# Maxima across partitions by turns on TensorE, row sums on ScalarE, keys split ahead, and a projection placed inside the first layer

## The reference

```python
q, k, v = (einsum('blh,dh->bdl', u, W) + b for W, b in ((Wq, bq), (Wk, bk), (Wv, bv)))
k  = causal_conv(k, k_kernel) + k_D[None, :, None] * k       # by FFT of length 1024, first 512 kept
kv = k * v
y  = (causal_conv(kv, ssm_kernel) + kv * D[None, :, None]) * q
x  = layernorm(u + einsum('blh,oh->blo', swapaxes(y, 1, 2), Wo) + bo)
h  = square(relu(einsum('bsd,fd->bsf', x, W_fc)))            # 256 -> 1024
s  = einsum('bsf,df->bsd', h, W_proj)                        # 1024 -> 256
spikes: 5 steps of mem = 0.9 * mem + s - reset; count of mem > 1, divided by 5
out = layernorm(x + spikes / 5)
```

## Time and profile before

| | us |
|---|---|
| median of 3 runs (lowest to highest) | 859.67 (856.86 to 860.92) |
| profiled execution: time, span | 861.3, 859.3 |
| TensorE busy (share of the span) | 743.8 (87%) |
| VectorE busy | 713.3 (83%) |
| ScalarE busy | 529.9 (62%) |
| GpSimd busy | 390.3 (45%) |
| mean granted TensorE clock | 0.962 of full |

### The profile page before, as it was taken

The page is one execution under the profiler, slowest core; times in us unless marked ns, Lnnn a source line. Parts: engine busy times, 40 slices in busy tenths (PEclk is TensorE's granted clock), DMA queues, the critical chain, the costliest instruction groups (busy, mean ns, idle before and its releaser), DMA issues.

```text
span 859.3 us, 26944 instructions
## 1 busy us (share of the span) xinstructions
PE 743.8 (87%) x11392; PEld 545.7 (64%) x11392; DVE 713.3 (83%) x1192; ACT 529.9 (62%) x625; POOL 390.3 (45%) x307
## 2 busy tenths in 40 slices
PE   0067977999999999766699999999999999999993
PEld 0067977999999999765455555555555455555541
DVE  6896755788888888886568999999999999999885
ACT  2382746778878887765255655666555665556661
POOL 0341212223222222322377666876668866677642
PEclk9998988999999999986799999999999999999997
DMA  8994857999999997890100111011110111101001
GB/s 336 342 263 103 189 135 173 210 231 224 222 228 227 226 211 160 187 263 20 49 1 1 50 49 49 5 44 49 49 49 11 37 49 49 49 20 31 25 24 50
DMA packets 55369, 100.71 MB, mean 117 GB/s; under 512 B 5664, under 2 KB 41376, under 8 KB 53280
## 3 DMA queue, kind: packets, MB, share of 16 engines
q1 hardware_dynamic: 53952, 97.94, 44.7%
q10 hardware_dynamic: 1376, 2.23, 0.7%
HBM read 89.92 MB, written 27.01 MB: 136 GB/s over the span
## 4 chain that ended last, share of the span: by engine, by line
PE 44%; DVE 24%; POOL 17%; issue 10%; DMA 2%; ACT 1%; SPq 0%; POOLq 0%; DVEq 0%; ACTq 0%
PE ps L697 16%; PE ps L683 15%; POOL arena L630 14%; DVE arena L1184 7%; PE ps L813 5%; PE ps L820 5%; DVE u_maxima L917 2%; DVE arena L1181 2%; PE ps L794 2%; DVE arena L1141 2%; DVE arena L1166 2%; DVE arena L1160 2%; DVE arena L971 1%; DMA arena<-kpad_dram 1%; PE ps L772 1%
## 5 line engine op out<-in xcount | busy, mean ns | idle before, releaser
L683 PE MATMUL ps<-arena 128*128 128x96 f16 x3072 | 143.2, 211 | 62.2 <-DVE arena L971 50.8
L697 PE MATMUL ps<-arena 128*128 128x64 f16 (+3 forms) x6144 | 172.2, 182 | 23.3 <-issue 8.9
L630 POOL TENSOR_TENSOR arena<-arena 128x512 f16<-128x512 f32 x128 | 178.9, 1429 | 14.9 <-ACT arena L514 14.4
L697 PEld LDWEIGHTS ps<-arena 128*128 128x128 f16 x6144 | 169.7, 97 | 24.5 <-issue 14.7
L683 PEld LDWEIGHTS ps<-arena 128*128 128x128 f16 x3072 | 138.4, 101 | 64.6 <-issue 56.4
L820 PE MATMUL ps<-arena 128*128 128x512 f16 x768 | 173.2, 379 | 2.9 <-POOL arena L630 2.9
L813 PE MATMUL ps<-arena 128*128 128x512 f16 x768 | 170.8, 379 | 3.4 <-DVE arena L1166 2.5
L596 POOL TENSOR_TENSOR arena<-arena 128x512 f16<-128x512 f32 x32 | 38.1, 1190 | 240.4 <-ACT arena L471 240.4
L1173 DVE TENSOR_TENSOR arena<-arena 128x512 f32<-128x512 f32 x128 | 137.7, 1129 | 10.8 <-POOL arena L630 9.0
L510 ACT ACTIVATE arena<-ps,read_factor 128x512 f32<-128x512 f32 x128 | 88.0, 687 | 76.6 <-PE ps L813 59.6
L820 PEld LDWEIGHTS ps<-arena 128*128 128x128 f16 x768 | 74.0, 98 | 90.6 <-POOL arena L630 9.7
(11 more groups left out here) (99 smaller groups left out, 724.9 us busy)
## 6 DMA issues: line engine op xcount, KB each, us to landing
arena<-kpad_dram SPq DMA_DIRECT2D x192, 256.0 KB, 5.8
kpad_dram<-ksplit_dram SPq DMA_DIRECT2D x64, 256.0 KB, 6.2
qy<-in_uT SPq DMA_DIRECT2D x8, 1024.0 KB, 17.2
arena<-in_u SPq DMA_DIRECT2D x16, 512.0 KB, 4.0
out<-arena SPq DMA_DIRECT2D x16, 512.0 KB, 3.0
arena<-in_k SPq DMA_DIRECT2D x2, 512.0 KB, 5.1
ksplit_dram<-arena ACTq DMA_DIRECT2D x2, 512.0 KB, 3.7
arena<-in_wfT SPq DMA_DIRECT2D x1, 1024.0 KB, 8.7
```

Of the source, the lines that this page charges most:

```text
L630: nc.gpsimd.tensor_tensor(h16[:, 1, f], h_square[:, f % 4], h16[:, 0, f], ALU.subtract).then_inc(h_lo, 1)
L683: last = nc.tensor.matmul(o, u16[:, x, t, tok:tok + P], wcur[:, w, t], start=(k == 0), stop=(k == 3 * DT - 1))
L697: last = nc.tensor.matmul(out[:, ch * COL + delta * B:(ch + 1) * COL], taps(c, tp)[:, delta * P:(delta + 1) * P], data[:, xp, ch * COL:ch ...
```

## The change

1. The three `partition_all_reduce` go. In their place TensorE turns the columns of maxima (n columns become n rows), VectorE takes the maximum of each row and spreads it over 128 columns (`spread_max`), TensorE turns that back, and VectorE copies it out of PSUM. For the third of them the banks are those of `turn_y`, so `turn_y(0)` waits for `all_max2_read`.
2. ScalarE makes the row sums (Abs with `accum_out`, six instructions); VectorE takes the three maxima of them.
3. ScalarE and GpSimd split the keys of g+1 before the products of g, and ScalarE's wait is for the keys alone (`keys_read`, raised before the queries and values are read).
4. SP issues `wfT` and `wpT` one group earlier, and `wo`, `bo` and two pieces of `u` at group NG-3, ahead of the last windows.
5. The gather of sequence 0 is halved between ScalarE and VectorE. VectorE makes the first residual sum and its moments tile by tile, from `wo_first`, which `project_out(0)` raises twice.
6. `project_out(1)` moves from ahead of `turn_x(0)` into `body(0)`, behind four parts of the up-projection; in that body VectorE's `first_sum(1)` comes after the fourth square and `norm_shift` after the seventh.

Buffers and semaphores that are only declared are left out:

```diff
@@ -372,15 +385,15 @@
                         load_windows2(s + 1, half)
+                if s == NG - 5:
+                    sp.dma_start(wf_st, wfT.rearrange("(t p) n -> p t n", p=P)).then_inc(ld_wf, 16)
                 if s == NG - 4:
-                    sp.dma_start(wf_st, wfT.rearrange("(t p) n -> p t n", p=P)).then_inc(ld_wf, 16)
+                    sp.dma_start(wp_st, wpT.rearrange("(t p) n -> p t n", p=P)).then_inc(ld_wp, 16)
                 if s == NG - 3:
-                    sp.dma_start(wp_st, wpT.rearrange("(t p) n -> p t n", p=P)).then_inc(ld_wp, 16)
-            sp.dma_start(wo, woT.rearrange("(t p) n -> p t n", p=P)).then_inc(ld_wo, 16)
-            sp.dma_start(bo_b[:, 0:D], bo.partition_broadcast(P)).then_inc(ld_wo, 16)
-
-            def load_u(b, r):
-                sp.dma_start(u_bo[:, r], u[bass.ds(b * NI, NI)].rearrange("i p n -> p i n")).then_inc(ld_u_seq[r], 16)
+                    sp.dma_start(wo, woT.rearrange("(t p) n -> p t n", p=P)).then_inc(ld_wo, 16)
+                    sp.dma_start(bo_b[:, 0:D], bo.partition_broadcast(P)).then_inc(ld_wo, 16)
+                    load_u(0, 0)
+                    load_u(1, 1)
@@ -390,8 +403,6 @@
-            load_u(0, 0)
-            load_u(1, 1)
             next_u(2, 0)
@@ -418,6 +429,16 @@
             nc.scalar.activation(*as_pairs(causal, step_st), ACT.Copy).then_inc(causal_done, 1)
+
+            def add_rows(src, size, n):
+                nc.scalar.activation(row_junk[:, n, 0:size], src, ACT.Abs, accum_out=row_sums[:, n:n + 1]).then_inc(row_sums_done, 1)
+
+            act.wait_ge(ld_w, 48)
+            for n in range(2 * DT):
+                add_rows(wn_st[:, n // DT, n % DT], D, DT + n)
+            act.wait_ge(taps_ready, 1)
+            for n in range(DT):
+                add_rows(k_st[:, 0, n], L, n)
             act.wait_ge(scales1, 1)
@@ -451,7 +472,7 @@
             def k_part(g):
-                act.wait_ge(proj_read, GPC * (g // GPC + 1))
+                act.wait_ge(keys_read, GPC * (g // GPC + 1))
                 if g >= 1:
@@ -467,10 +488,10 @@
             def step(s, g):
+                if g + 1 < NG:
+                    k_part(g + 1)
                 act.wait_ge(kv_ready, g + 1)
                 nc.scalar.activation(kv16[:, s % 2, 0], kv, ACT.Copy).then_inc(kv_hi, 1)
-                if g + 1 < NG:
-                    k_part(g + 1)
                 if 0 < g < NG - 1:
@@ -538,7 +559,7 @@
             act.wait_ge(y_ready, NG)
-            nc.scalar.activation(y_seq[:, 0], y_by_token[:, :, :, 0], ACT.Copy).then_inc(y_first_ready, 1)
+            nc.scalar.activation(y_seq[:, 0, 0:2], y_by_token[:, 0:2, :, 0], ACT.Copy).then_inc(y_first_ready, 1)
             y_turn(0)
@@ -573,18 +594,12 @@
             nc.gpsimd.tensor_copy(ident16[:, :], ident[:, :]).then_inc(id_done, 1)
-            pool.wait_ge(part_max_done, 1)
-            nc.gpsimd.partition_all_reduce(all_max[:, 0:NST], part_max[:, 0:NST], P, bass.bass_isa.ReduceOp.max
-                                           ).then_inc(all_max_done, 1)
             pool.wait_ge(w_hi, 1)
...
                                         ).then_inc(kpad_lo, 1)
-            pool.wait_ge(u_maxima_done, 1)
-            nc.gpsimd.partition_all_reduce(u_max[:, :], u_maxima[:, NU:NU + 1], P, bass.bass_isa.ReduceOp.max
-                                           ).then_inc(u_max_done, 1)
@@ -592,10 +607,10 @@
             def step(s, base, more):
+                if not (isinstance(base, int) and base + s == NG - 1):
+                    k_part(s + 1, base + s + 1)
                 pool.wait_ge(kv_hi, base + s + 1)
                 nc.gpsimd.tensor_tensor(kv16[:, s % 2, 1], kv, kv16[:, s % 2, 0], ALU.subtract).then_inc(kv_lo, 1)
-                if not (isinstance(base, int) and base + s == NG - 1):
-                    k_part(s + 1, base + s + 1)
@@ -701,6 +713,17 @@
+            def cross_max(src, n, nth, ready, done):
+                pe.wait_ge(ready, 1)
+                nc.tensor.transpose(ps[0:n, 6, 0:P], src, ident[:, :]).then_inc(turned0, 1)
+                pe.wait_ge(spread0, nth + 1)
+                nc.tensor.transpose(ps[:, 7, 0:n], spread_max[0:n, :], ident[0:n, 0:n]).then_inc(done, 1)
+
+            pe.wait_ge(id_done, 3)
+            cross_max(part_max[:, 0:NST], NST, 0, part_max_done, all_max_done)
+            pe.wait_ge(max_read, 1)
+            cross_max(u_maxima[:, NU:NU + 1], 1, 1, u_maxima_done, u_max_done)
+            pe.wait_ge(max_read, 2)
             pe.wait_ge(ld_wcur, 16)
@@ -766,6 +789,12 @@
+            pe.wait_ge(id_done, 3)
+            pe.wait_ge(part_max2_done, 1)
+            nc.tensor.transpose(ps[0:3, 0, 0:P], part_max[:, cF:cF + 3], ident[:, :]).then_inc(turned2, 1)
+            pe.wait_ge(spread2, 1)
+            nc.tensor.transpose(ps[:, 1, 0:3], spread_max[0:3, :], ident[0:3, 0:3]).then_inc(all_max2_done, 1)
+
             def turn(src, done):
@@ -793,7 +822,10 @@
                                                 wo[:, t], start=(t == 0), stop=(t == DT - 1))
-                last.then_inc(wo_done, 1)
+                    if isinstance(i, int) and i == 0 and j % 2:
+                        last.then_inc(wo_first, 1)
+                if not (isinstance(i, int) and i == 0):
+                    last.then_inc(wo_done, 1)
@@ -854,10 +886,13 @@
             def body(i, r, left):
-                if left and not (isinstance(i, int) and i == 0):
+                first = isinstance(i, int) and i == 0
+                if left and not first:
                     project_out(i + 1)
                 up(i, r, range(0, 4))
-                if not (isinstance(i, int) and i == 0):
+                if first:
+                    project_out(i + 1)
+                else:
                     turn_counts(i - 1, left)
@@ -920,27 +955,36 @@
+            nc.vector.memset(cell[:, 0:1], 0.0).then_inc(taps_ready, 1)
             for c in range(2):
                 max_abs(part_max[:, cK1 + c:cK1 + c + 1], k_st[:, c])
-            max_of_row_sums(cL1, k_st[:, 0], DT)
             dve.wait_ge(ld_w, 48)
             max_abs(part_max[:, cW:cW + 1], w_st)
-            max_of_row_sums(cLK, wn_st[:, 0], DT)
-            max_of_row_sums(cLV, wn_st[:, 1], DT)
+            dve.wait_ge(row_sums_done, 3 * DT)
+            for n, col in enumerate((cL1, cLK, cLV)):
+                max_abs(part_max[:, col:col + 1], row_sums[:, n * DT:(n + 1) * DT], AX.X)
             dve.wait_ge(ld_b, 16)
...
-            dve.wait_ge(all_max_done, 1)
+            def cross_max(n, nth, dst, done):
+                dve.wait_ge(turned0, nth + 1)
+                link(nc.vector.tensor_reduce(scratch[0:n, 8:9], ps[0:n, 6, 0:P], AX.X, ALU.max))
+                nc.vector.tensor_copy(spread_max[0:n, :], scratch[0:n, 8:9].to_broadcast([n, P])).then_inc(spread0, 1)
+                dve.wait_ge(done, 1)
+                nc.vector.tensor_copy(dst, ps[:, 7, 0:n]).then_inc(max_read, 1)
+                dve.wait_ge(max_read, nth + 1)
+
+            cross_max(NST, 0, all_max[:, 0:NST], all_max_done)
             pow2(w_scale[:, 0:3], w_unscale[:, 0:3], all_max[:, 0:3], scratch[:, 0:3])
...
             nc.vector.tensor_reduce(u_maxima[:, NU:NU + 1], u_maxima[:, 0:NU], AX.X, ALU.max).then_inc(u_maxima_done, 1)
-            dve.wait_ge(u_max_done, 1)
+            cross_max(1, 1, u_max[:, :], u_max_done)
             pow2(d_scale[:, 0:1], d_unscale[:, 0:1], u_max[:, :], scratch[:, 0:1])
@@ -993,7 +1037,7 @@
                 dve.wait_ge(proj, n + 1)
-                read_scaled(0, kbuf, quarter, r, chunk, banks)
+                read_scaled(0, kbuf, quarter, r, chunk, banks).then_inc(keys_read, 1)
                 dst = quarter_of(qy[:, bass.ds(chunk * CH * COL, CH * COL)], quarter)
@@ -1115,7 +1159,14 @@
             times_q(PAIR - 1, NG - 1)
+            dve.wait_ge(y_ready, NG)
+            nc.vector.tensor_copy(y_seq[:, 0, 2:4], y_by_token[:, 2:4, :, 0]).then_inc(y_first_ready, 1)
+            dve.wait_ge(turned2, 1)
+            link(nc.vector.tensor_reduce(scratch[0:3, 8:9], ps[0:3, 0, 0:P], AX.X, ALU.max))
+            nc.vector.tensor_copy(spread_max[0:3, :], scratch[0:3, 8:9].to_broadcast([3, P])).then_inc(spread2, 1)
             dve.wait_ge(all_max2_done, 1)
+            nc.vector.tensor_copy(all_max[:, 3:6], ps[:, 1, 0:3]).then_inc(all_max2_read, 1)
+            dve.wait_ge(all_max2_read, 1)
             pow2(w_scale[:, 3:6], w_unscale[:, 3:6], all_max[:, 3:6], scratch[:, 0:3])
@@ -1193,7 +1244,18 @@
-            first_sum(0, 0)
+            dve.wait_ge(u_bo_ready, 1)
+            for j in range(NI):
+                dve.wait_ge(wo_first, j // 2 + 1)
+                last = nc.vector.tensor_tensor(sum1[:, j], PN[:, j], u_bo[:, 0, j], ALU.add)
+                last.then_inc(sum_first, 1)
+                dve.wait_ge(sum_first, j + 1)
+                last = nc.vector.bn_stats(bn_parts[:, 0, j], sum1[:, j])
+                last.then_inc(moments_first, 1)
+                dve.wait_ge(moments_first, j + 1)
```

(9 more changed lines are left out.)

35 lines of the change are left out of this document (22 added, 13 removed).

## The result

| | before | after |
|---|---|---|
| median (lowest to highest), us | 859.35 (856.86 to 860.92) | 867.78 (866.71 to 868.41) |
| ratio, 95% interval | | 1.009 (1.0071 to 1.0109) |
| profiled execution: time, span | 861.3, 859.3 | 867.55, 865.8 |
| granted TensorE clock | 0.962 | 0.955 |

The change makes the kernel slower, by 8.4 us between the medians and by 7.7 us (0.9%) by the ratio. The forecast was 863.2 us, range 856.5 to 867.5, no change the likeliest: the time is 0.3 us above the range, and it is slower.

What follows compares the result with a forecast made beforehand. It took VectorE to set the time in prologue and tail, GpSimd to be late at the change of stage, TensorE nearly full elsewhere. 0.5 + 0.4 + 2.6 = +3.5 us on 861.3; by the median 863.2, range 856.5 to 867.5.

Steps and rivals of the forecast that it cites:

- layer 1's root ahead of layer 0's low halves: First layer: GpSimd's order puts VectorE's first down-projection step 27.3 us after the up-projection begins; +2.6 us net.
- The change of stage: From convolution stage to layer stage: the first up-projection starts at 418.9, 6.35 us sooner, all given back in the first layer.
- The prologue: Kernel start, until 48 us, where VectorE alone sets the time: +0.5 us, bounds -0.5 to +2.8.
- row sums: Prologue: ScalarE makes six instead of VectorE's three; `part_max` complete at 16.95 against 16.54, +0.4 us, bounds 0 to +2.6.
- turns: Prologue: TensorE's turns at 0.3 and 0.2 us, 1.45 us per maximum across partitions; +0.85 for the first, -0.73 for the second.
- Rival C: Change of stage's gain survives, second projection costing only its own 3.6 us: -5.2 us, 854.5 us; chance 0.16.
- rival D: No change at all: gains and losses past the prologue cancel, +0.5 us, 860.2 us; chance 0.10.
- rival B: First layer: TensorE's clock falls while it is fed slowly, later work at half clock; +6.8 us, 866.5 us; chance 0.22.
- GpSimd's wait for layer 1's moments: First layer, a sign to look for: GpSimd waits about 10 us for these moments.
- the tail: End of the convolution stage: copies near 0, load queue a little worse, keys ahead 0; +0.4 us, bounds -3.0 to +3.0.
- the steady part: Convolution stage, 165 to 350 us: TensorE has no wait that splitting keys ahead ends; 0 us.
- three signs: Forecast wrong if up-projection to down-projection step is under 24 us, row sums end after 17, or steady part shows over 3 us.

Runs made afterwards that it cites:

- the three repairs: Kernel after with the second projection outside the first layer, loads at their old places, gathers held until the third scales are made: 855.97 us, ratio 0.9956.
- the last experiment: The three repairs with the first maximum across partitions back on GpSimd, the second still by turns: 854.26 us, ratio 0.9940.

## Why the prediction was wrong, step by step

**Right.** The mechanism that the forecast put its sum on: layer 1's root ahead of layer 0's low halves. From up-projection to spikes it said 27.3 us; 27.11 came. The change of stage was to gain 6.35 us by itself; it gained 6.39. The prologue was to cost 0.5 in bounds of -0.5 to +2.8; it cost 0.24: row sums cheaper (`part_max` complete at 16.28, not 16.95), turns dearer (0.37 and 0.28 us where 0.3 and 0.2 were taken, each maximum 1.60 to 1.62 instead of 1.45). Rival C asked for 22 us from up-projection to spikes (18.3 + 3.6), rival D for no more than 24.7 (18.3 + 6.35), and both fall.

**Right by luck in part.** The 27.3 us hide two errors that cancel. The root took 1.3 us (436.40 to 437.69), not 2.2: the forecast had taken the longer of two roots of the kernel before, and the one at its change of stage, at 413.98, took 1.3. From the last low half (448.49) to the spikes it is 1.13 us and not 0.4; before it was 0.66, and 0.48 with the loads back. There a part of rival B came true (slower by the clock inside the first layer): after waits of 0.77 and 1.03 us the granted clock was 0.69 from 445.9 to 448.5 us and 0.50 to 450.2, and 18 matmuls of the down-projection took 5.75 us where the kernel with the loads back needs two times 2.12. That is some 0.65 us of stretch D (1.13 less 0.48) and not rival B's 3.3 us: what came later ran at full clock again (the projection at 454.15, 3.62 us). And GpSimd's wait for layer 1's moments, "about 10 us" in the forecast, was 20.68, of which 13.9 lie behind the start of the up-projection.

**The step that failed is the tail.** "Copies near 0, queue a little worse" was +0.4; it was +2.16 in the profiled execution. The mechanism, a fuller queue of loads, was named; its size was wrong. The two parts, loads and keys, were sized wrongly in opposite directions. The loads cost 3.0 us of B and 3.4 of the time in the kernel after (1.5 alone); I had named +2.1 as the end of the range and taken the middle. The row already showed VectorE waiting for taps with one load of 1 MB ahead of them, and the change put 1.4 MB more ahead of the next ones. The keys gained 1.4 to 1.5 in the tail, where I had taken 0. With keys ahead VectorE meets late taps more often: in the tail of the three repairs it waits 1.24, 0.85 and 2.93 us, and 2.92 once without. That this is why the loads are dearer in the kernel after than alone is likely and not shown.

**A block on the path that I had not priced.** The third maximum's spread copy took 1.64 us instead of 0.21, beside GpSimd's gather. I had weighed such meetings for the long copies of the tail only. The first projection started 1.0 us later for it (7.0 us behind the last query product instead of 6.0) and ran partly at full clock, 5.21 us instead of 6.66. Neither set the time: VectorE, late with its split of the weights, made the four sums from 410.28 to 414.34, so that the moments were there 15.1 us behind the last query product and not 14.4, and the root took 1.3 us and not 2.2. So the change of stage came out as forecast by errors that cancelled.

**What stays open.** The forecast gave the steady part nothing; A is 1.49 us later, of which the prologue gives 0.24. From 48 to 97 us the kernel after is 1.0 us faster, and from 97 to 148 us it loses 2.1, in TensorE's waits without a shown releaser:

```profile
125.17 6.41 PE L709 MATMUL ps<-arena 128*128 128x64 f16 x192 [4.68 <-issue]
140.77 6.80 PE L709 MATMUL ps<-arena 128*128 128x64 f16 x192 [4.59 <-issue]
```

Before has 3.58 and 3.79 there, 7.37 together. But the two together are 8.86 with the projection inside before, whose code up to there is that of before, and between 7.65 and 9.27 in the eight kernels with keys ahead. So executions differ by as much as is to be explained: no edit is shown to bring these 1.25 us, and which instruction is waited for was not found. That term of the sum, 0, is neither shown nor refuted.

**The sum once more.** Forecast +3.5 = 0.5 (prologue) + 0.4 (tail) + 2.6 (change of stage and first layer). Profiled: 0.24 + 1.25 (open) + 2.16 + 2.38 = +6.03. Between the medians it is 8.4, since the profiled execution of before lay 1.9 us above its median and that of after 0.2 below. None of the three signs that the forecast named as its own refutation came, and it was wrong all the same: they watched the prologue, the steady part and the first layer, and none watched the queue of loads. With a sum of +3.5 and a line at +4.3, 0.35 was a small chance for slower.

## What to carry to other kernels

A projection that is moved to save time must be followed into each queue that it feeds: here it went to a place where GpSimd's, VectorE's and ScalarE's queues hold the same layer's work behind its result. Alone that gave 3.19 us at the change of stage, took 9.0 in the first layer and made the kernel 6.6 us slower; and with the rest of the change its old place cost nothing, since it fills 3.69 of 5.76 us in which TensorE waits anyway. Loads for a later stage belong behind the last loads of a stage that already waits for its own. The faster route for a small reduction depends on what stands around it: the same maximum across partitions cost VectorE 0.60 us by GpSimd the first time and 1.20 to 2.18 the second time, against 1.6 by turns both times. And when a meeting of two engines is moved, it has to be asked what it meets next: the gathers held up one small step, then two, then a long one, each time on the way to the first residual sum.

## What the runs showed of the hardware that I had not expected

- A VectorE instruction on three elements per partition can last as long as a GpSimd copy of 1024: 1.86 and 1.91 us instead of 0.17 for scale steps, 1.64 instead of 0.21 for a spread copy. The Trainium skill ("SBUF — State Buffer", SBUF: two separate sides) states that a VectorE instruction in a two-port mode and a GpSimd instruction shut each other out for a whole instruction; the traces agree (the held copy ends at 402.49, the gather at 402.40), though none shows which mode the small steps ran in, and they show that the smallest instructions can pay the whole price.
- Around `partition_all_reduce` GpSimd stands idle on both sides. Behind it, before the next ordinary instruction, it was 6.7 to 7.6 us (7.61 and 7.15 before, 6.72 with the new prologue alone, 7.16 in the last experiment); in front of it, behind an ordinary instruction, 5.6 to 6.5 us (6.48 and 5.94 before). The trace of the kernel before has two MODIFY_POOL_CONFIG on GpSimd's queue at the start of each of these gaps (17.1, 32.2, 391.2 and 397.2 us); those for the first reduction stand at 2.6 us, and that one answered in 0.60. So what takes the time goes, as these rows read, with the change between the two kinds of instruction. With turns on TensorE `add_bo` follows the last product at once (394.44).
- TensorE's isolated 32-bit turns last 0.37 us for 11 columns of 128 partitions and 0.28 for the turn back; each of the first two maxima takes 0.56 and 0.35 to 0.37 us of VectorE's waiting for them.
- ScalarE's sum with an accumulator is two instructions, 0.40 and 0.19 us for 256 elements, and a pair starts every 0.40 us (0.61 for 512).
